# Key order swapped for half of the head pairs, six turnings per sequence instead of eight, and feed-forward rows turned three blocks ahead

## The reference

```python
h = einsum('bsk,kh->bsh', concat(pos_emb, nest_emb, seg_emb), W)
# attention, 8 heads of 64, on x = layernorm(h)
q, k, v = x @ wq + bq, x @ wk + bk, x @ wv + bv
logits = where(k_index <= q_index, (q / 8) . k, -1e10)     # with 128 tokens the mask is plainly causal
h = h + softmax(logits) . v @ wo + bo
# experts: top 2 of 8, on x = layernorm(h)
cw = softmax of the two best router logits
h1, h2 = split(x @ fc1[e].T + fc1_b[e])                    # 2 x 256
h = h + sum over the two e of cw[e] * ((silu(h1) * h2) @ fc2[e].T + fc2_b[e])
```

## Time and profile before

| | |
|---|---|
| median of 3 runs | 1257.07 us (1255.15 to 1257.45) |
| the profiled execution | 1256.33 us, of which the span from first to last instruction is 1254.6 us |
| mean granted TensorE clock | 0.974 of full speed |
| busy: TensorE, VectorE, ScalarE, GpSimd | 1172.8, 993.3, 992.7, 755.2 us |
| attention | up to about 826 us |
| table, first loads | to 847.6 us, TensorE idle for 15.2 us |
| feed-forward, two passes | 847.6 us to the end, with one gap where pass 0 drains and pass 1 loads (from about 1041 to 1051 us) |

### The profile page before, as it was taken

The page is one execution under the profiler, slowest core; times in us unless marked ns, Lnnn a source line. Parts: engine busy times, 40 slices in busy tenths (PEclk is TensorE's granted clock), DMA queues, the critical chain, the costliest instruction groups (busy, mean ns, idle before and its releaser), DMA issues. The chain is left out here.

```text
span 1254.6 us, 45360 instructions
## 1 busy us (share of the span) xinstructions
PE 1172.8 (93%) x13125; PEld 1031.4 (82%) x13126; DVE 993.3 (79%) x3799; ACT 992.7 (79%) x3491; POOL 755.2 (60%) x1082
## 2 busy tenths in 40 slices
PE   6899999999999999999999999729999997999996
PEld 4578888888888888888888887619999996999995
DVE  6568988888888888888888887756777774777774
ACT  2799999999999999999999998726666664666663
POOL 6436755565565555565565555544777774777775
PEclk9899999999999999999999999968999998999998
DMA  5151110100100111110010111115666663555552
GB/s 177 60 186 56 39 35 32 43 32 32 47 32 32 43 36 32 42 37 32 32 43 32 36 43 40 53 53 170 197 206 199 203 191 130 159 143 143 159 153 68
DMA packets 68049, 108.97 MB, mean 87 GB/s; under 512 B 12756, under 2 KB 32948, under 8 KB 67860
## 3 DMA queue, kind: packets, MB, share of 16 engines
q1 hardware_dynamic: 50068, 62.67, 17.7%
q0 software_dynamic: 17920, 45.55, 10.0%
HBM read 45.66 MB, written 54.11 MB: 80 GB/s over the span
## 5 line engine op out<-in xcount | busy, mean ns | idle before, releaser
L764 ACT ACTIVATE probs<-ps,neg_max 128x128 f32<-128x128 f32 (+1 forms) x1024 | 337.8, 363 | 2.0 <-DVE neg_max L961 1.9
L764 ACT ACTIVATION_READ_ACCUMULATOR probs<-ps,neg_max 128x1 f32 x1024 | 236.3, 231 | 0.0
L574 POOL TENSOR_TENSOR probs<-probs,inv_sums 128x384 f32<-128x384 f32 x120 | 99.2, 826 | 205.4 <-DVE inv_sums L910 205.4
L1143 DVE SCALAR_TENSOR_TENSOR probsT<-ps,b_now,masked 128x256 f32<-128x256 f32 x286 | 125.3, 480 | 85.5 <-PE ps L1237 66.0
L1235 PE MATMUL ps<-xT_hi,w_now 128*128 128x256 f32 x572 | 173.1, 303 | 0.8 <-DVE xT_lo L1127 0.8
L720 ACT ACTIVATE masked<-ps,b_now 128x256 f32<-128x256 f32 x286 | 119.8, 471 | 59.5 <-PE ps L1237 59.1
L1237 PE MATMUL ps<-xT_hi,w_now 128*128 128x256 f32 x572 | 162.8, 285 | 0.0
L1236 PE MATMUL ps<-xT_lo,w_now 128*128 128x256 f32 x572 | 161.9, 283 | 0.0
L631 POOL DMA_INDIRECT xs<-normed,row x128 | 137.0, 1070 | 41.2 <-issue 36.9
L1418 PE MATMUL ps<-w,probsT 128*128 x1144 | 150.8, 275 | 0.0
L1363 PEld LDWEIGHTS ps<-probsT,v 128*64 128x64 f32 x2048 | 109.8, 137 | 45.2 <-issue 44.4
(11 more groups left out here) (243 smaller groups left out, 3181.8 us busy)
## 6 DMA issues: line engine op xcount, KB each, us to landing
v<-xs SPq DMA_DIRECT2D x108, 260.0 KB
kT<-xs SPq DMA_DIRECT2D x35, 260.0 KB
xs<-pad_rows SPq DMA_DIRECT2D x16, 520.0 KB, 3.4
normed<-h SPq DMA_DIRECT2D x32, 256.0 KB, 2.6
w_parts<-in_w SPq DMA_DIRECT2D x1, 2048.0 KB, 8.9
xs<-normed,row POOLq DMA_INDIRECT x128, 2.7
xs<-v POOLq DMA_INDIRECT x108
out_h<-v POOLq DMA_INDIRECT x108
```

The costliest lines, as they stand in the source:

```text
L764: ins = nc.scalar.activation(probs_p[par][:, half, slots[n]], ps[:, SCORES + half, slots[n]], ACT.Exp, bias=neg_max[par][:, half, n:n + 1] ...
L1143: V.scalar_tensor_tensor(actT[z][:, f], ps[:, H2[z], f * BLK:(f + 1) * BLK], b1_now[j % WBUFS][:, 2 + f:3 + f], gate[z][:, f], ALU.add, AL ...
```

## The change

- `kT` is written with the two halves of a sequence's keys swapped for head pairs 1 and 3. A lower piece of such a pair then has its 64 keys where the turning puts them on partitions 64 to 127, so one turning of 128 columns takes two lower pieces at once (`turned_at`). The pieces of a bank change places, three turnings per half remain, and PSUM needs no zeros any more.
- `v` must have the same key order: its columns for pairs 1 and 3 are computed with swapped rows, by three matmuls instead of one (one on the whole array, two on half of its columns).
- The 1/deviation is now multiplied into `v`, by a new GpSimd step `vscale` (128x512, once per sequence), which needs it in a second, swapped copy (two VectorE copies of 64x4 in `norm`, once per group); `rstd_now` goes.
- ScalarE's copies of turned probabilities are 384 columns instead of 512, without a scale.
- `mix` is 16 matmuls of 64 queries: first eight of 64 keys on quarters of the array, then eight of 128 keys on halves. Its output lies in two banks, one of them that of the turned half 1.
- In the feed-forward, rows are turned three blocks ahead (`AHEAD`), and the turned rows have four pairs of buffers.

The core of the diff:

```diff
+AHEAD = 3
...
             late("route_weight", half - 2)
+        steps.append(("vscale", half + 1, n))
         late("scatter", half - 3, n, n + 1)
...
-        slots = (slice(0, S), slice(S + HQ, 2 * S + HQ), slice(S, S + HQ), slice(2 * S + HQ, PACK))
+        slots = (slice(0, S), slice(2 * S, PACK), slice(S, S + HQ), slice(S + HQ, 2 * S))
+        turned_at = (slice(0, S), slice(S, 2 * S), slice(2 * S, PACK))
...
-        x3_hi = [xT_hi[0][:, 0:BLK], xT_hi[1][:, 0:BLK]]; x3_lo = [xT_lo[0][:, 0:BLK], xT_lo[1][:, 0:BLK]]
+        x3_hi = [t[:, m * BLK:(m + 1) * BLK] for t in xT_hi for m in range(2)]; x3_lo = [t[:, m * BLK:(m + 1) * BLK] for t in xT_lo for m in range(2)]
...
-                    pool.wait_ge(rstd_ready, LEAD + G + 1)
-                    pool.wait_ge(pTb_ready, LEAD + GB * (G - 1))
+                elif kind == "vscale":
+                    G, n = 2 * o + i, st[2]
+                    pool.wait_ge(v_ready, LEAD + GB * G + n + 1)
+                    pool.wait_ge(rstd_put, LEAD + 2 * (G + 1))
                     carry_wait(pool)
-                    pool.tensor_copy(rstd_now[i % 2][:], rstd[i % 2][:]).then_inc(rstd_put, 1)
+                    rows = v[i % 2][:, n].rearrange("p (c n d) -> p c n d", c=2, n=2)
+                    pool.tensor_tensor(rows, rows, rstd[i % 2][:, n].unsqueeze(1).broadcast_to([S, 2, 2]).unsqueeze(3).broadcast_to([S, 2, 2, 128]),
+                                       ALU.mult).then_inc(v_scaled, 1)
...
-                act.wait_ge(h2_full, LEAD + n - 1)
-                nc.scalar.copy(x3_hi[z], ps[:, XB[z], 0:BLK]).then_inc(x3hi_ready, 1)
+                act.wait_ge(h2_full, LEAD + n + 1 - len(x3_hi))
+                nc.scalar.copy(x3_hi[j % len(x3_hi)], ps[:, XB[j % 2], 0:BLK]).then_inc(x3hi_ready, 1)
...
-                        nc.scalar.activation(kT[par][:, pair], ps[:, KEY], ACT.Identity, bias=bias_qk[:, 1, pair:pair + 1],
-                                             scale=1.0).then_inc(qk_ready, 1)
+                        keys = ps[:, KEY].rearrange("p (j a c) -> p j a c", j=GB, a=2)
+                        nc.scalar.activation(kT[par][:, pair].rearrange("p (j a c) -> p j a c", j=GB, a=2), keys[:, :, ::-1] if pair % 2 else keys,
+                                             ACT.Identity, bias=bias_qk[:, 1, pair:pair + 1], scale=1.0).then_inc(qk_ready, 1)
...
-                    nc.scalar.activation(probsT[:, 0:4], ps[:, PROBST].rearrange("p (n k) -> p n k", n=4), ACT.Identity,
-                                         scale=rstd_now[gp][:, j:j + 1]).then_inc(pTa_ready, 1)
+                    nc.scalar.copy(probsT[:, 0:3].rearrange("p n k -> p (n k)"), ps[:, PROBST, 0:PACK]).then_inc(pTa_ready, 1)
...
+                    dve.wait_ge(v_scaled, LEAD + GB * (G - 1))
+                    carry_wait(dve)
+                    for c in range(2):
+                        V.tensor_copy(rstd[par][(1 - c) * HQ:(2 - c) * HQ, :, 1], rstd[par][c * HQ:(c + 1) * HQ, :, 0]).then_inc(rstd_put, 1)
...
-                    T.matmul(ps[:, VALUE], onehot[par][:, j * S:(j + 1) * S], v_table[:], start=True, stop=True).then_inc(v_full, 1)
+                    T.matmul(by_pair(ps[:, VALUE])[:, :, 0], onehot[par][:, j * S:(j + 1) * S], by_pair(v_table[:])[:, :, 0], start=True, stop=True)
+                    for c in range(2):
+                        ins = T.matmul(by_pair(ps[(1 - c) * HQ:(2 - c) * HQ, VALUE])[:, :, 1], onehot[par][:, j * S + c * HQ:j * S + (c + 1) * HQ],
+                                       by_pair(v_table[:])[:, :, 1], start=True, stop=True)
+                    ins.then_inc(v_full, 1)
...
+                    pe.wait_ge(mixT_ready, LEAD + b)
+                    for part in turned_at:
+                        ins = T.transpose(ps[:, PROBST + 1, part], probs_p[par][:, 1, part], ident[:])
                     ins.then_inc(pTb_full, 1)
...
-                        pe.wait_ge(v_ready, LEAD + GB * (2 * o + i // GB + 1))
+                        pe.wait_ge(v_scaled, LEAD + GB * (2 * o + i // GB + 1))
                     pe.wait_ge(mixT_ready, LEAD + b)
                     pe.wait_ge(pTa_ready, LEAD + b + 1)
                     pe.wait_ge(pTb_ready, LEAD + b + 1)
-                    for pair in range(PAIRS):
-                        for e in range(2):
-                            head = 2 * pair + e
-                            ins = T.matmul(ps[e * HD:(e + 1) * HD, MIX, pair * S:(pair + 1) * S], v[gp][:, j, head * HD:(head + 1) * HD],
-                                           probsT[:, e * PAIRS + pair], start=True, stop=True)
+                    carry_wait(pe)
+                    for part in (1, 0):
+                        for c in range(2):
+                            for n in range(2):
+                                for e in range(2):
+                                    heads = slice((4 * c + 2 * n + e) * HD, (4 * c + 2 * n + e + 1) * HD)
+                                    keys, queries, at = ((slice(0, S), HQ, 2 * n), (slice(n * HQ, (n + 1) * HQ), 0, 1))[part]
+                                    ins = T.matmul(ps[e * HD:(e + 1) * HD, MIX - 1 + n, c * S + queries:c * S + queries + HQ], v[gp][keys, j, heads],
+                                                   probsT[keys, e * PAIRS + at, c * HQ:(c + 1) * HQ], start=True, stop=True)
                     ins.then_inc(mix_full, 1)
...
                 if not last:
-                    rows_in(n + 2, i + (j + 2) // XBUFS, (j + 2) % XBUFS)
+                    rows_in(n + AHEAD, i + (j + AHEAD) // XBUFS, (j + AHEAD) % XBUFS)
```

More of the change, by code:

```diff
@@ L65, in octet_steps @@
             steps.extend(("value", 0, n) for n in range(GB))
+            steps.extend(("vscale", 0, n) for n in range(GB))
             steps.append(("onehot", 2))
@@ L724, in block_of @@
                 if not last:
-                    halve(n + 2, z)
+                    halve(n + AHEAD, j + AHEAD)
             def step(o, st, opening=False):
@@ L819, in _ @@
             for k in range(TOPK):
-                for n in range(2):
+                for n in range(AHEAD):
                     halve(k * PH + n, n)
@@ L829, in _ @@
                 for n in range((k + 1) * PH - XBUFS, min((k + 1) * PH, LAST + 1)):
-                    block_of(n, n % XBUFS, experts, last=(n + 2 > (PH - 1, LAST)[k]), ahead=(n + WBUFS - 1 <= LAST))
+                    block_of(n, n % XBUFS, experts, last=(n + AHEAD > (PH - 1, LAST)[k]), ahead=(n + WBUFS - 1 <= LAST))
         @block.vector
@@ L1181, in turn @@
                         give(k, before, XBUFS - 1)
-                    if not last or n + 2 <= (PH - 1, LAST)[k]:
-                        rest(n + 2, j % 2)
+                    if not last or n + AHEAD <= (PH - 1, LAST)[k]:
+                        rest(n + AHEAD, j + AHEAD)
             dve.wait_ge(s_w1hi, EXPERTS)
@@ L1327, in step @@
                                 rows, pair = slice(e * HD, (e + 1) * HD), 2 * c + n % 2
+                                keys = slice(at, at + S) if high else slice(at + HQ * (n % 2), at + HQ * (n % 2) + HQ)
                                 ins = T.matmul(ps[c * HQ:(c + 1) * HQ, SCORES + e, slots[n]], qT[gp][rows, pair, at + high * HQ:at + high * HQ + HQ],
-                                               kT[gp][rows, pair, at:at + (S if high else HQ)], start=(n == 0), stop=False, skip_group_check=True)
+                                               kT[gp][rows, pair, keys], start=(n == 0), stop=False, skip_group_check=True)
                     for e in range(2):
                         rows = slice(e * HD, (e + 1) * HD)
-                        masked_keys = ps[:, SCORES + e, 0:PACK].rearrange("p (a k) -> p a k", a=2)[:, :, HQ:S + HQ]
-                        ins = T.matmul(masked_keys, ident_2[rows].rearrange("p c q -> p (c q)"), causal[rows].rearrange("p a n k -> p a (n k)"), start=False, stop=True,
+                        masked_keys = ps[:, SCORES + e, HQ:HQ + 2 * S]
+                        ins = T.matmul(masked_keys, ident_2[rows].rearrange("p c q -> p (c q)"), causal[rows].rearrange("p a n k -> p (a n k)"), start=False, stop=True,
                                        skip_group_check=True)
@@ L1343, in step @@
                     pe.wait_ge(pTa_ready, LEAD + b)
-                    for n in range(4):
-                        ins = T.transpose(turned(0, n), probs_p[par][:, 0, slots[n]], ident[:])
+                    for part in turned_at:
+                        ins = T.transpose(ps[:, PROBST, part], probs_p[par][:, 0, part], ident[:])
                     ins.then_inc(pTa_full, 1)
@@ L1465, in _ @@
                 for n in range((k + 1) * PH - XBUFS, min((k + 1) * PH, LAST + 1)):
-                    block_of((k + 1) * turns - 1, n % XBUFS, last=(n + 2 > (PH - 1, LAST)[k]))
+                    block_of((k + 1) * turns - 1, n % XBUFS, last=(n + AHEAD > (PH - 1, LAST)[k]))
                 e = pe.value_load(table_e[0:1, n:n + 1], min_val=0, max_val=EXPERTS - 1)
```

68 lines of the change are left out of this document (35 added, 33 removed).

## The result

The changed kernel takes 1300.99 us (median of four runs, 1296.28 to 1302.65) against 1257.26 us for the kernel before: ratio 1.0344, 95% interval 1.0319 to 1.0369. The forecast was 1281 with a range to 1300. The direction and the place were right, the size was not: 44 us lost where 24 were forecast. The profiled execution spans 1298.7 us against 1254.6.

A forecast was written before the change was run, and what follows sets the result against it. TensorE was taken as the bound, with VectorE and ScalarE nearly tight. 1256.3 us, less 6 for TensorE, plus 27 for the hold and 3 for the feed-forward, gave 1280, as median 1281; 8-in-10 range 1238 to 1300.

The forecast's parts named there:

- The hold: Second sequence of a group: vscale on GpSimd holds VectorE 0.85 to 1.05 us, taken 0.95; 28 groups, +27 us.
- the once-per-group wait: TensorE idles once per group before the fourth sequence's scores at 424.03, released by ScalarE's exponentials, 0.95 us later.
- the copies: Two new 64x4 VectorE copies in the second sequence: between 0 and 0.32 us each, taken 0.17 for both.
- TensorE's per sequence: TensorE's net change per sequence: -0.07 us, bounds -0.5 and +0.6.
- turnings: TensorE's turnings per sequence, three instead of four per half: taken -0.22 us.
- values: TensorE's values, three matmuls instead of one with two array changes: bounds 0 and +0.3, taken +0.2 us a sequence.
- mix: TensorE's mix with 64-column passes and one extra change of array shape: taken -0.05 us a sequence.
- 93 sequences: Sequences that TensorE was taken still to pace, each gaining 0.07 us: 6 us less in the sum.
- Feed-forward: Rows needed one block sooner, two or three TensorE waits up to 1.5 us: +3 us, bounds 0 and +27.
- slower by TensorE: Mix halves at 68 ns or shape changes twice 0.08: +0.3 us a sequence without any hold, 1297 us; chance 0.15.
- Faster: VectorE not held on its path, vscale late or line 982 free; TensorE's gain shows, 1239 us; chance 0.2.

The follow-up runs named there:

- values_again: Repeat: changed kernel with the values in two matmuls of 256 columns, both of one array shape; ratio 1.0180 to the kernel before.
- mix_order: Changed kernel with the mix's two parts exchanged, the 64x64 part last; 1290.85 us, ratio 1.0272 to the kernel before.
- ffn_again: Kernel before with only the feed-forward part changed (rows turned three blocks ahead), on a quick chip; 1263.05 us, ratio 1.0050.
- ffn_only: Kernel before with only the feed-forward part changed (rows turned three blocks ahead), on a chip with late loads; ratio 1.0127.
- behind: Changed kernel with the second sequence's scaling of v behind the scatter in GpSimd's queue; ratio 1.0526 to the kernel before.
- copies_act: Changed kernel with the second sequence's v scaling behind scatter and residual, and the two 64x4 copies on ScalarE; ratio 1.0214 to the kernel before.
- all5: Changed attention, v scaling behind the residual, one-shape values, mix's 64x64 part last, 64x4 copies on ScalarE, feed-forward as before; ratios 0.9905, 0.9885, 0.9878.
- attn_only: Changed kernel with the feed-forward put back to rows turned two blocks ahead; ratio 1.0225 to the kernel before.
- values_full: Changed kernel with the values in two matmuls of 256 columns, both of one array shape; ratio 1.0196 to the kernel before.
- before_hold: Kernel before with one GpSimd 128x512 multiply added per group, in the second sequence behind the token numbers; ratio 1.0047.
- copies_again: Repeat of copies_act, the same kernel on a chip with late loads; ratio 1.0195 to the kernel before.

## Why the prediction was right in kind and short in size

- **The hold and the once-per-group wait: right, the fit of the number partly luck.** 27 us were forecast for 28 third sequences at 0.95; they measure 0.99 in the steady octets and 29.8 us in all. The parts were off in opposite ways: the hold is 0.69 to 0.74, not 0.95 (GpSimd takes 1.05 us, forecast 1.1; line 996 is not held here, only the last centred row), the copies 0.39, not 0.17. The path was another one too: the wait was forecast at the fourth sequence's scores, released by ScalarE, and it shows ahead of line 1287, released by VectorE's line 981.
- **The step that failed: the mis-sized term is TensorE's per sequence.** "Sum -0.22 - 0.05 + 0.2 = -0.07 us". Measured: turnings -0.22 (0.49 to 0.38 and 0.44 to 0.33), values +0.21 and mix -0.02, all near; but project +0.10, which had no term. I took 0.08 for a change of how the array is cut. It is 0.10 to 0.11 in place, and 0.05 to 0.10 more in the matmuls that follow, where the weight load behind the change is not covered. So +0.08 us a sequence, not -0.07. Nor do 93 sequences carry it: the first and second of a group do, with 4.7 us in octets 1 to 14, the fourth shows 0.1. +5 in place of -6 is 11 of the missing 20 us. values_again and mix_order show the price by taking changes out.
- **The octets I did not look at.** The sum's hold was for octets 1 to 14. Start, octet 0, the last octet and the table bring 3.5 us without a term, and octet 1 4.0 where 1.9 stood: its third sequences take 8.3 and 8.8 us, before 6.4 and 6.8, beside GpSimd's split of the weights.
- **Feed-forward: right in kind, half in size.** +3 forecast, +6 measured (ffn_again +5.8): not three dips but some 20, most of them small.
- **The rival "slower by TensorE" had a good part of the truth** (a change costs about twice 0.08, with what follows it) and got 0.15. That its 1297 us lies close to the 1301 is luck: it has 0.3 us in every sequence and no hold, and neither is so. "Faster" fell with the hold: `vscale` started at once, as the earlier trace rows said it would. My forecast and that rival are not alternatives; they add. With the measured 5 in place of -6 the forecast's sum would be 1257 + 5 + 27 + 3 = 1292, inside the range and nearer than 1281. Treating them apart left the top of the range too low.

## What to carry to other kernels

Count the changes of how the array is cut in an order of matmuls as instructions of their own, here 0.1 us in place and up to as much again behind, before the columns saved are believed: the two changes at the values cost 0.31 us a sequence, and two turnings fewer gave 0.22. An instruction handed to an idle GpSimd can be paid for by VectorE, here 0.7 us of one of 1.05, where VectorE works from SBUF at that moment. What helped was to place it behind an instruction that itself waits for VectorE, not just later in the queue. And where several small losses are each plausible, add them; rivals that can hold at once do not share one chance.

## What the runs showed of the hardware that I had not expected

- An instruction of GpSimd that stands ready behind an indirect DMA holds VectorE's two-input instruction before it starts itself: 2.13 us for one of 0.56, in four runs, all on chips with late loads.
- On the three chips with late loads TensorE's completion of the mask matmul is signalled 1.0 to 1.4 us after its start instead of 0.30, in one sequence of four, while GpSimd puts out the scatter, though the matmuls go on in time. That is so in ffn_only, behind, copies_act and all5 and their repeats; in attn_only, values_full, values_again and before_hold, on the same chips, it is 0.30. ffn_only is the one kernel seen on both kinds: 0.99 us there, and 0.30 as ffn_again on the quick chip. VectorE's maxima then start 0.42 us behind the scatter's end (432.50 and 432.92 in copies_again). In the profile before, with scatter and maxima in the same positions, they do not the earlier trace rows. The cause is not known.
- The same three chips take 532 to 564 us for a feed-forward that takes 406 to 415 in the other profiles.
- With rows turned three blocks ahead, TensorE's granted clock over the feed-forward is 0.88 on such a chip (ffn_only) and 0.97 on the quick one (ffn_again), at the same work.
